# First routed tiles of a mixture-of-experts decoder layer: slot copies moved to ScalarE, tile 2 transposed amid the first gate-up

## The reference

```python
x = x + attention_over_the_batch(layernorm(x))
x = x + cross_attention(layernorm(x), ctx, mask, Wq, Wk, Wv, Wo, q_norm, k_norm)
x = x + ffn(layernorm(x), gate_w, bias, Wg, Wu, Wd, Sg, Su, Sd)

def ffn(x):                                  # 16 experts of 256 inner columns, top 4
    scores = sigmoid(x @ gate_w.T) + bias
    topk_w, topk_idx = top_k(scores, 4)
    topk_w = topk_w / (sum(topk_w) + 1e-20)
    cw = sum(one_hot(topk_idx, 16) * topk_w[..., None], axis=1)
    z = silu(einsum('th,eih->eti', x, Wg)) * einsum('th,eih->eti', x, Wu)
    out = einsum('eti,ehi->th', z * cw.T[:, :, None], Wd)
    return out + (silu(x @ Sg.T) * (x @ Su.T)) @ Sd.T
```

## Time and profile before

| | us |
|---|---|
| median of 3 runs | 809.94 (808.97 to 810.89) |
| the profiled execution's own time | 809.31 |
| its span, first to last instruction | 807.5 |
| TensorE busy | 777.2 (96%) |
| VectorE busy | 591.6 (73%) |
| ScalarE busy | 516.8 (64%) |
| GpSimd busy | 543.3 (67%) |

### The profile page before, as it was taken

One profiled execution on the slowest core, in us unless ns is written; L12 is line 12 of the kernel. 1 busy time (PEld: TensorE's weight loads), 2 busy tenths in 40 slices (PEclk: granted clock), 3 DMA queues, 4 the chain that ended last, 5 costly groups with the idle time before them and its releaser, 6 DMA issues.

```text
span 807.5 us, 21596 instructions
## 1 busy us (share of the span) xinstructions
PE 777.2 (96%) x7887; PEld 445.1 (55%) x7887; DVE 591.6 (73%) x1023; ACT 516.8 (64%) x968; POOL 543.3 (67%) x428
## 2 busy tenths in 40 slices
PE   6789999999999999999999999999998999999997
PEld 2664545645645655655654654654554565665653
DVE  5787795595685686777667668699688776767778
ACT  3898987487587587587578578636433566555551
POOL 6953496896896986976977978872253656565433
PEclk9799999999999999999999999999999999999999
DMA  8029516516507507516515524436515557678894
GB/s 329 18 95 290 164 67 235 143 53 227 165 26 234 164 18 238 168 36 229 158 55 188 176 79 151 124 113 248 177 52 209 199 182 248 219 282 277 264 401 183
DMA packets 50661, 138.94 MB, mean 172 GB/s; under 512 B 6176, under 2 KB 8224, under 8 KB 46240
## 3 DMA queue, kind: packets, MB, share of 16 engines
q1 hardware_dynamic: 43600, 116.93, 43.6%
q0 software_dynamic: 6400, 20.98, 7.6%
q10 hardware_dynamic: 592, 0.08, 0.1%
HBM read 96.02 MB, written 39.85 MB: 168 GB/s over the span
## 4 chain that ended last, share of the span: by engine, by line
PE 62%; POOL 13%; issue 8%; DVE 5%; DMA 5%; ACT 4%; SPq 2%; DVEq 0%; POOLq 0%; ACTq 0%
PE ps L1742 33%; PE ps L2192 18%; POOL ring_mem L623 4%; DMA stage<-in_wq 3%; POOL reg_h L661 3%; POOL ring_mem L609 2%; PE ps L2182 2%; POOL reg_h L665 2%; PE ps L1961 2%; POOL ring_mem L616 1%; PE ps L2253 1%; PE ps L1947 1%; PE ps L2207 1%; DMA w_split<-stage 1%; PE ps L1902 1%
## 5 line engine op out<-in xcount | busy, mean ns | idle before, releaser
L1742 PE MATMUL ps<-wo_hi,reg_b 128*128 128x512 f16 x448 | 142.5, 379 | 1.0 <-DVE x_res L1336 1.0
L2192 PE MATMUL ps<-ring_mem,reg_h 128*64 x480 | 116.6, 379 | 4.1 <-DVE kv L1639 2.3
L703 POOL DMA_INDIRECT y_rows<-reg_h,to_row x40 | 66.7, 1669 | 77.3 <-ACT reg_h L1115 71.6
L661 POOL TENSOR_SCALAR reg_h<-reg_h 128x512 f32<-128x512 f32 x56 | 95.4, 1704 | 33.2 <-ACT reg_h L913 33.0
L2194 PE MATMUL ps<-kv,reg_h 128*64 128x512 f16 x480 | 116.7, 380 | 0.0
L665 POOL TENSOR_TENSOR reg_h<-reg_h 128x512 f16<-128x512 f32 x84 | 108.7, 1294 | 4.7
L1742 PE MATMUL ps<-hT_hi,wq_hi 128*128 128x512 f16 x256 | 97.2, 380 | 2.0 <-DVE ring_mem L1279 1.8
L1742 PE MATMUL ps<-hT_hi,wq_lo 128*128 128x512 f16 x256 | 97.2, 380 | 0.0
L1742 PE MATMUL ps<-hT_lo,wq_hi 128*128 128x512 f16 x256 | 97.1, 379 | 0.0
L623 POOL TENSOR_TENSOR ring_mem<-kv,ring_mem 128x512 f16<-128x512 f32 x64 | 80.3, 1255 | 24.2 <-ACT ring_mem L838 24.2
L1742 PE MATMUL ps<-wo_lo,reg_b 128*128 128x512 f16 x224 | 85.0, 379 | 0.0
(11 more groups left out here) (343 smaller groups left out, 2019.2 us busy)
## 6 DMA issues: line engine op xcount, KB each, us to landing
ring_mem<-w_split SPq DMA_DIRECT2D x16, 1536.0 KB, 7.7
w_split<-reg_h SPq DMA_DIRECT2D x88, 256.0 KB, 2.1
reg_h<-in_wgu SPq DMA_DIRECT2D x58, 256.0 KB, 3.6
stage<-in_wq SPq DMA_DIRECT2D x8, 1024.0 KB, 8.9
stage<-in_wo SPq DMA_DIRECT2D x8, 1024.0 KB, 6.6
reg_h<-in_wd SPq DMA_DIRECT2D x30, 256.0 KB, 3.1
wkv_st<-in_wkv SPq DMA_DIRECT2D x8, 512.0 KB, 9.5
ring_mem<-in_x_half SPq DMA_DIRECT2D x8, 256.0 KB, 6.1
```

Of the source, the lines that this page charges most:

```text
L661: pool.tensor_scalar(st, st, WS, None, ALU.mult).then_inc(pre_scaled_pool, 1)
L703: pool.indirect_dma_start(y_rows, bass.IndirectOffsetOnAxis(ap=to_row[:, r - 1:r], axis=0), y[r % 2], None).then_inc(scattered[r % 2], 16)
L1742: last = pe.matmul(dst, lhsT(c), rhs(c), start=(m == 0), stop=(m == n - 1))
L2192: pe.matmul(dst[0:TS, :], x[:, 0:TS], ring[:, bass.ds(at + w, BANK)], start=(first and n == 0), stop=(stop and n == 2))
```

## The change

1. In the shared units ScalarE makes the high part of unit 0 before the Silu of unit 1, and that of unit 1 before the Silu of unit 2.
2. ScalarE copies both halves of the slot rows for tiles 1, 2 and 3 (`slots_hi` and the new `slots_lo`); VectorE copies the low half from tile 4 on. For tile 2 ScalarE does it before the Silu of tile 1.
3. The gate copy of tile 1 is made in two halves, each with an increment of `upper_loaded`, so all later counts are one higher. `gate_up(1)` waits for the first half alone. `gate_up(2)` waits for three increments, that is for its own gate copy.
4. `transpose_slots(2)` stands in the middle of `gate_up(1)`, ahead of the second half of its products; it also waits for the second half copy. In `gate_up(2)`, `turn_gated(1)` stands before the last quarter and not in the middle.
5. The five table products stand one shared down unit earlier.
6. At the end a second pick product stands before the last down products.

```diff
--- before.py
+++ after.py
@@ -1072,10 +1072,10 @@
                     act.wait_ge(z32_done, u - 1)
                 act.activation(silu[:, u % 2, :], ps[:, 2 * (u % 3), :], ACT.Silu, scale=1.0 / WS).then_inc(silu_done, 1)
 
-            for u in range(3):
+            for u in range(2):
                 shared_silu(u)
-                if u >= 1:
-                    z_hi_part(u - 1)
+                z_hi_part(u)
+            shared_silu(2)
             act.wait_ge(onehots, 1)
             for t in range(NT):
                 ks = slice(t * TOPK, (t + 1) * TOPK)
@@ -1118,14 +1118,24 @@
 
                 act.activation(factors(t, k), ident[:, :], ACT.Copy, scale=wk[:, t, k:k + 1]).then_inc(factors_done, 1)
 
+            def slots_lo(r):
+                act.wait_ge(tT_ps, r)
+                act.activation(tT[r % 2][:, 1, :, :], ps[:, 5, :].rearrange("p (k s) -> p k s", k=KC),
+                               ACT.Copy).then_inc(tT_lo_done, 1)
+
             slots_hi(1)
-            act.activation(tT[1][:, 1, :, :], ps[:, 5, :].rearrange("p (k s) -> p k s", k=KC), ACT.Copy).then_inc(tT_lo_done, 1)
+            slots_lo(1)
             for r in range(1, TILES + 1):
+                if r == 1:
+                    slots_hi(r + 1)
+                    slots_lo(r + 1)
                 if r >= 2:
                     gated_turned(r - 1)
                 gated(r)
-                if r < TILES:
+                if 1 < r < TILES:
                     slots_hi(r + 1)
+                if r == 2:
+                    slots_lo(r + 1)
                 gated_hi(r)
                 if r >= 2:
                     down_out(r - 1)
@@ -1632,7 +1642,11 @@
 
                 dve.wait_ge(ready, loads)
                 dve.nop(nofuse=True)
-                dve.tensor_copy(upper_w[r % 2][:, 0:2 * BANK * KC], ring[:, bass.ds(at, 2 * BANK * KC)]).then_inc(upper_loaded, 1)
+                parts = 2 if r == 1 else 1
+                n = 2 * BANK * KC // parts
+                for part in range(parts):
+                    dve.tensor_copy(upper_w[r % 2][:, part * n:part * n + n],
+                                    ring[:, bass.ds(at + part * n if part else at, n)]).then_inc(upper_loaded, 1)
 
             def upper_down(r, at):
 
@@ -1703,11 +1717,9 @@
                     rows_done, 1)
 
             for r in range(1, TILES + 1):
-                if 1 < r < TILES:
+                if 3 <= r < TILES:
                     slots_lo(r + 1)
                 gated_up(r)
-                if r == 1:
-                    slots_lo(r + 1)
                 gated_lo(r)
                 for t, k in MID_SUMS.get(r, ()):
                     token_sum(t, k)
@@ -2159,7 +2171,7 @@
                     last = pe.matmul(ps[:, 7, k * TILES:(k + 1) * TILES], on_b[:, TOPK * t + k, :],
                                      on_tok[:, TOPK * t + k, :], start=(t == 0), stop=(t == NT - 1))
             last.then_inc(slot_ps, 1)
-            for t in range(2, NT - 1):
+            for t in range(2, NT - 2):
                 shared_down(t)
             pe.wait_ge(tab_done, 1)
             pe.wait_ge(rows_done, 2)
@@ -2209,7 +2221,7 @@
                 last.then_inc(zT_ps, 1)
 
             def gate_up(r, at):
-                pe.wait_ge(upper_loaded, 2 * r - 1)
+                pe.wait_ge(upper_loaded, {1: 1, 2: 3}.get(r, 2 * r))
                 pe.wait_ge(tT_hi_done, r)
                 pe.wait_ge(tT_lo_done, r)
                 if r <= 2:
@@ -2218,7 +2230,10 @@
                     pe.wait_ge(z32_done, SHARED_UNITS + r - 2)
                 hi, lo = tT[r % 2][:, 0, :, :], tT[r % 2][:, 1, :, :]
                 for k in range(KC):
-                    if k == KC // 2 and r >= 2:
+                    if k == KC // 2 and r == 1:
+                        pe.wait_ge(upper_loaded, 2)
+                        transpose_slots(2)
+                    if k == (KC - 1 if r == 2 else KC // 2) and r >= 2:
                         turn_gated(r - 1)
                     last = half_products(r, ps[:, r % 2, :], hi[:, k, :], lo[:, k, :], k, at, k == 0, k == KC - 1)
                 last.then_inc(gu_ps, 1)
@@ -2229,12 +2244,13 @@
                     pe.wait_ge(d_added, NT)
                 if r >= 3:
                     pe.wait_ge(y_done, r - 2)
-                pe.wait_ge(upper_loaded, 2 * r)
+                pe.wait_ge(upper_loaded, 4 if r == 1 else 2 * r + 1)
                 for c in range(IC):
                     last = half_products(r, ps[:, 6 + r % 2, :], zT[r % 2][:, 0, c, :], zT[r % 2][:, 1, c, :], KC + c, at,
                                          c == 0, c == IC - 1)
                 last.then_inc(td_ps, 1)
 
+            shared_down(NT - 2)
             transpose_slots(1)
             shared_down(NT - 1)
             pe.wait_ge(tables_done, 1)
@@ -2256,8 +2273,9 @@
             pe.wait_ge(factors_done, len(FACTOR_ORDER))
             pick_product(*FACTOR_ORDER[0])
             turn_gated(TILES)
+            pick_product(*FACTOR_ORDER[1])
             down(TILES, before_at)
-            for t, k in FACTOR_ORDER[1:]:
+            for t, k in FACTOR_ORDER[2:]:
                 last = pick_product(t, k)
                 if k == PE_PICKS[t][-1]:
                     last.then_inc(y_summed, 1)
```

## The result

| | before | after |
|---|---|---|
| median of 20 runs each, us | 810.25 (807.5 to 814.71) | 807.71 (805.38 to 811.89) |
| profiled execution's own time | 809.31 | 805.38 |
| its span | 807.5 | 803.5 |
| TensorE busy | 777.2 (96%) | 775.6 (97%) |
| VectorE / ScalarE / GpSimd busy | 591.6 / 516.8 / 543.3 | 590.1 / 517.8 / 540.8 |

The ratio after to before is 0.9968, with a 95% interval of 0.9957 to 0.9978: 2.6 us faster, between 1.8 and 3.5. The forecast was 2.4 us and 807.5.

A forecast was written before the change was run, and what follows sets the result against it. TensorE was taken to bound the loop, so only its gaps can be won: 1.95 at the loop's start plus 0.4 at the end makes 2.35, say 2.4 us, for a median of 807.5 us; range 806.7 to 809.1.

The forecast's parts named there:

- the forecast's own signs of being wrong: Product at 581.57 over 1 us, cast no earlier than 603.7, TensorE idle after 750, gate-up 1 waiting for ScalarE beyond 606.5.
- Step 1: Shared units: ScalarE's earlier high parts move GpSimd's low parts off VectorE's small operation; 0.5 us earlier.
- rival 2: Shared units: GpSimd comes first at 581.57 and shuts out VectorE's product; gain only 1.35, 808.6 us; chance 0.20.
- rival 1: Shared units give nothing, VectorE meeting GpSimd elsewhere for as long; gain 1.9, 808.0 us; chance 0.20.
- Step 2: Earlier tables, halved gate copy of tile 1: cast at 603.26, gate-up 1 at 606.2 instead of 607.58, 1.38 us sooner.
- Step 3: Transposes of tile 2 amid gate-up 1: gate-up 2 starts at 609.7 instead of 613.15.
- Step 4: VectorE's chain to tile 3's gate copy: gate-up 3 at 615.9 instead of 617.94; 1.95 us for the loop's start.
- Step 5: Kernel end: second pick fills TensorE's wait before the last down products, removing VectorE's 0.41 wait; 0.4 us.
- Rival 3: Later in the loop, something not following TensorE, such as the last expert loads, takes the gain back; 809.5 us; chance 0.06.

The follow-up runs named there:

- x1: Changed kernel with ScalarE's old order in the shared units (each high part one Silu later): median 807.92 us of 8 runs, ratio to before 0.9974.
- x6: Changed kernel with the table products one shared down unit later again, as before the change: 810.82 us in one profiled execution.
- v1: Changed kernel with the token weight product moved from the routing chain to VectorE's work of tile 3: median 808.85 us of 12 runs, ratio to before 0.9982.
- x5: Changed kernel with the gate copy of tile 1 in one piece: 808.32 us in one profiled execution.
- x7: Kernel before with only gate-up 2 waiting for its own gate copy, no longer for the down copy of tile 1: 808.06 us in one profiled execution.
- x2: Changed kernel with gate-up 2 waiting again for the down copy of tile 1: 808.13 us in one profiled execution.
- x3: Changed kernel with the low slot copies of tiles 2 and 3 back on VectorE: 808.10 us in one profiled execution.
- x4: Kernel before with only the second pick product put ahead of the last down products: 809.11 us in one profiled execution.
- v3: v2 with VectorE's remaining routing work (scatter counts, token weights) two tiles later: median 806.90 us of 12 runs, ratio to before 0.9964.
- x6b: Second run of the x6 kernel, table products one shared down unit later than in the changed kernel: 807.64 us in one profiled execution.
- v2: v1 with the row table of the scatters moved behind VectorE's low part of tile 2: median 807.90 us of 12 runs.

## Why the prediction was right, and where it was not

**Time and bound: right, the number in part by luck.** 2.4 us were forecast, 2.6 (1.8 to 3.5) measured, at most 1.9 counted in one pair of traces. The two gaps that went and the one that stays came as said. But three of the forecast's own signs of being wrong came too: the weight product took over 1 us (1.27), the cast came no earlier than 603.7 (23.60 is 603.72 counted from before's zero), and gate-up 1 waited for ScalarE's copies beyond 606.5 (606.70). What the measured time has over the counted share lies within the interval, and single executions differ by more than that before the zero and in the loop.

**Step 1, the shared units: wrong.** Forecast 0.5 us earlier, measured nothing (x1: 0.05 apart). The failed sentence is the one in rival 2 that GpSimd "seems to need about 0.14 of its 1.15 us before it excludes anyone". It was read from one pair of rows in which VectorE had started first, and such a pair can't tell a start-up from plain order. The place was rival 2's, with the product at 1.27 for 0.29. The size was rival 1's, "VectorE meets GpSimd elsewhere for as long as before": it put the cast at 603.74 and gate-up 1 at 606.65. Rival 2 had the table 0.6 late, but later meetings paid part back. The operation that follows MAX8 went from 0.18 to 0.42, and the second one-hot of the chain from 2.65 to 2.28 us, so the sum over the stretch is +0.98 − 0.80 + 0.24 − 0.37 = +0.05. The Trainium skill (SBUF — State Buffer, Who interferes with whom) has whichever issues first hold the shared port for its whole instruction; the rows agree with it, with a lead of 0.03 us deciding over 0.98 us. So the two engines meet here too, and not through semaphores alone.

**Step 2, cast and gate-up 1: right but for what step 1 left.** Cast forecast at 23.14 after the zero, measured 23.60. The 0.40 us gained against before is the tables' (x6: 0.4 inferred). S1 forecast at 26.08, measured 26.58. Of the two paths to it, which the forecast had end together, ScalarE's was the later. The early table products waited 0.30 for VectorE's late table, so the transposes of tile 1 began 24.47 after the zero and not at the 23.89 where they were to stay. ScalarE's second copy then ended at 604.38, 26.23 after the zero, and TensorE started 0.35 later:

```profile
603.79 0.59 ACT L1123 ACTIVATE reg_h<-ps 128x512 f16<-128x512 f32 x1
```

The forecast had 0.44 for that last handover, from the one row of gate-up 3. With the table as early as forecast or earlier (v1), the transposes are back at 23.91 and S1 is 26.04. Halving the copy is worth 0.48 (x5); the first half took 0.69, against the 0.70 taken. The forecast's "24 pairs" of a gate-up are 24 products in 12 pairs, of which 6 stand ahead of the transposes; its 2.60 and 1.30 us are right.

**Step 3, tile 2 amid gate-up 1: right.** S2 − S1 forecast 3.5, measured 3.40.

**Step 4, what is late next: right in place and near in size.** S3 − S2 forecast 6.2, measured 6.24; the wait before gate-up 3 forecast at over 1 us, measured 1.13; S3 came at 36.22, forecast at 35.78, again step 1. Tile 4 took back 0.02 where 0.1 was subtracted. The parts aren't additive: the relaxed wait gives 0 alone (x7) and 1.06 in the changed kernel (x2), the slots give 1.16 in the changed kernel (x3); without the relaxed wait they weren't tried. What decides is VectorE's chain up to the gate copy of tile 3.

**Step 5, the end: right up to the last sum, wrong behind it.** VectorE's wait of 0.41 went, as forecast, and the last sum ended 0.51 earlier; the other 0.10 is that the last two sums now run without a pause between them (1.28 for the pair). The forecast took that for the end of the kernel and left out the last store. Its landing took back 0.2 of the 0.51 in the changed kernel and all of it in x4.

**Sum.** 1.57 + 0.51 − 0.2 = 1.9 at most where 1.95 + 0.4 = 2.35 was forecast: 0.5 too much in step 1, 0.1 too little in step 4, and 0.1 to 0.4 too much in step 5. Rival 1 was thus the nearer account of the start (1.5 of its 1.9 are the loop's, 1.57 measured). Its 808.0 and the forecast's 807.5 can't be told apart by the times. Rival 3, a later loss of what was won, didn't happen in this pair: 0.09 us between gate-up 5 and tile 40. Why x1's scatters came late, and what the 1.26 us idle of TensorE is, stays open; neither was tried.

## What to carry to other kernels

When two engines share a port, moving one of them to "where the other is idle" needs the start times of both within some hundredths of a microsecond. If you can't have them, take the exposed operation off the critical chain (v1: 0.69 us at the cast, of which 0.34 are left at gate-up 5 and none is seen in the times). Where several waits end close together, price the pair and not each: the relaxed wait was worth nothing alone, and 1.06 us beside the other parts. An early place for the producer that everything waits for can also absorb a delay of its engine (1.1 us for 0.4), but only while the chain beside it has slack: with the weight product away (v3) the same delay came through. And follow a gain at the end to the last store's landing, not to the last sum.

## What the runs showed of the hardware

- A lead of 0.03 us of a GpSimd operation on 128 x 512 elements costs a VectorE product with both inputs in SBUF 0.98 us (1.27 for 0.29); one of 0.23 us costs a 16-column operation 0.79. One with an operand in PSUM lost nothing at a lead of 0.02 (0.42, v1).
- TensorE stood idle for 1.26 us with no releaser at one and the same place in 5 of 13 executions, among them two of the same kernel (x6, x6b), and v3, whose TensorE program is that of v2, which had none.
- The same code reached the zero between 578.15 and 582.42 us. That is more than the whole effect of the change, so two spans can't be compared without such a common mark.
- TensorE starts 0.13 us after a gate copy that is the last of its waits, and 0.35 to 0.44 us after a low slot copy, which in the listing of the kernel before is the first of them (0.35 at x2 and x3, 0.44 before).
- The last store landed later behind sums without a pause: SyncE waited 1.8 us for it before and 1.7 in x7, and 2.0 or 2.3 us in the 11 executions with the second pick product.
